# Attention scores of a two-block layer: fp32 matmuls on 32-row strips in place of bf16 stacks through DRAM

## The reference

```python
q, k, v = proj(layernorm(x), Wq, bq), proj(ctx, Wk, bk), proj(ctx, Wv, bv)   # 16 heads of 16
scores = jnp.clip(einsum('bhsd,bhtd->bhst', q, k) / 4, -50, 50)
scores = jnp.where(attend, scores, -10000.0)                                # then clipped to -50
probs = softmax(scores);  ctx = einsum('bhst,bhtd->bhsd', probs, v)
x = x + tanh(g) * layernorm(0.05 * (ctx @ Wo.T + bo))
```

## Time and profile before

| | |
|---|---|
| median of 3 runs | 513.97 us (513.65, 513.97, 520.17) |
| span of the profiled execution | 516.7 us, from the first to the last instruction |
| its own time | not listed apart; of the three runs only 520.17 us is above the span |
| TensorE matmul, weight loads | 366.7 us (71%), 247.4 us (48%) |
| VectorE, ScalarE, GpSimd | 364.3 us (71%), 191.3 us (37%), 154.6 us (30%) |
| mean granted TensorE clock | 0.867 |
| chain that ended last | TensorE 36%, VectorE 33%, issue 14%, ScalarE 7%, DMA 5% |

### The profile page before, as it was taken

The page is one execution under the profiler, slowest core; times in us unless marked ns, Lnnn a source line. Parts: engine busy times, 40 slices in busy tenths (PEclk is TensorE's granted clock), DMA queues, the critical chain, the costliest instruction groups (busy, mean ns, idle before and its releaser), DMA issues.

```text
span 516.7 us, 6750 instructions
## 1 busy us (share of the span) xinstructions
PE 366.7 (71%) x2192; PEld 247.4 (48%) x2192; DVE 364.3 (71%) x887; ACT 191.3 (37%) x336; POOL 154.6 (30%) x150
## 2 busy tenths in 40 slices
PE   4664965628998859795975788797686468660665
PEld 2342542405565648584853556565563235530333
DVE  3174875395653498988788656754998697789895
ACT  2333752222441412251334445453201658721231
POOL 5058058100002544554622541212601220030230
PEclk9796997756999998997998899998977879977685
DMA  8499999930111121330498491364100192000001
GB/s 193 134 139 167 148 189 262 266 52 0 42 27 35 62 82 29 94 120 3 119 187 175 92 165 59 59 105 87 18 0 1 47 150 30 2 1 0 20 11 51
DMA packets 47009, 44.20 MB, mean 86 GB/s; under 512 B 6304, under 2 KB 45952, under 8 KB 46976
## 3 DMA queue, kind: packets, MB, share of 16 engines
q1 hardware_dynamic: 44768, 40.53, 38.6%
q0 software_dynamic: 1152, 2.20, 1.8%
q10 hardware_dynamic: 1056, 1.05, 0.7%
HBM read 36.43 MB, written 7.34 MB: 85 GB/s over the span
## 4 chain that ended last, share of the span: by engine, by line
PE 36%; DVE 33%; issue 14%; ACT 7%; DMA 5%; POOL 3%; SPq 1%; DVEq 0%; ACTq 0%; POOLq 0%
PE bank L848 9%; PE bank L874 5%; PE bank L776 4%; DMA probs<-in_L_xattn_Wq 3%; PE bank L733 2%; DVE probs L1264 2%; DVE tok L1223 2%; PE bank L984 2%; PE bank L948 2%; DVE mxraw L1552 2%; DVE mam L1394 2%; DVE probs L1479 1%; PE bank L896 1%; PE bank L810 1%; DVE st L1208 1%
## 5 line engine op out<-in xcount | busy, mean ns | idle before, releaser
L874 PE MATMUL bank<-wexp,wT 128*128 128x256 f32 x192 | 56.1, 420 | 10.1 <-DVE x L1386 10.0
L848 PE MATMUL bank<-tok_r,probs_r 128*128 128x512 f32 x104 | 47.1, 453 | 10.2 <-DVE wT L1375 7.0
L1264 DVE TENSOR_SCALAR probs<-probs,hi 128x512 f32<-128x512 f32 x64 | 32.8, 564 | 28.8 <-ACT probs L1045 28.8
L1097 ACT ACTIVATE silu_sb<-bank 128x512 f32<-128x512 f32 x32 | 19.1, 598 | 86.2 <-PE bank L848 86.2
L659 POOL TENSOR_TENSOR wexp_r<-wexp,probs_r 128x1024 fp32r<-128x1024 f32 x13 | 31.3, 2405 | 58.6 <-ACT probs_r L1056 58.5
L874 PEld LDWEIGHTS bank<-wexp,wT 128*128 128x128 f32 x192 | 38.4, 211 | 17.6 <-issue 12.4
L1045 ACT ACTIVATE probs<-bank 128x1024 f32<-128x1024 f32 x32 | 32.3, 1027 | 38.2 <-PE bank L760 38.2
L584 POOL TENSOR_TENSOR mx_grid<-parts,bl 128x1024 bf16<-128x1024 fp8e4 x9 | 17.2, 1910 | 96.1 <-DVE parts L1555 96.1
L1479 DVE SCALAR_TENSOR_TENSOR probs<-bank,dexp 128x384 f32<-128x384 f32 x48 | 26.5, 555 | 21.7 <-PE bank L934 15.9
L848 PE MATMUL bank<-tok_r,wexp_r 128*128 128x512 f32 x104 | 41.7, 401 | 0.0
L569 POOL TENSOR_TENSOR mxraw<-mxraw,mx_grid 128x512 f32<-128x512 f32 x12 | 15.3, 1275 | 63.8 <-DVE mx_grid L1420 63.8
(11 more groups left out here) (243 smaller groups left out, 923.0 us busy)
## 6 DMA issues: line engine op xcount, KB each, us to landing
krep<-part_dram SPq DMA_DIRECT2D x64, 128.0 KB, 6.4
qrep<-part_dram SPq DMA_DIRECT2D x64, 128.0 KB, 6.7
wexp<-in_L_ffn_W SPq DMA_DIRECT2D x28, 256.0 KB, 4.4
part_dram<-parts SPq DMA_DIRECT2D x12, 384.0 KB, 3.6
wexp<-in_L_ffn_Wg SPq DMA_DIRECT2D x14, 256.0 KB, 4.4
part_dram<-parts POOLq DMA_DIRECT2D x4, 384.0 KB, 8.1
x<-in_x ACTq DMA_DIRECT2D x2, 512.0 KB, 9.6
ctx<-in_ctx SPq DMA_DIRECT2D x2, 512.0 KB, 9.7
```

The source lines that it names most:

```text
L848: mm = pe.matmul(bank[:, bk, :], lhs, rhs, start=(kk == 0 and q == 0), stop=(kk == KC - 1 and q == len(terms) - 1))
L874: mm = pe.matmul(bank[:, 2 + pair, D * t:D * t + D], hid[k % 2][m][:, col:col + P], wexp[:, k % WR, 2, m, :], start=(m == 0), stop=(m == 1))
L1097: act.activation(silu_sb[:, w % 2, :], bank[:, 0, :], ACT.Silu if direct else ACT.Tanh, scale=1.0 if direct else 0.5).then_inc(s["sigmoid_ ...
L1264: ins = v.tensor_scalar(w, w, hi[:, 2 * b + kc:2 * b + kc + 1], EM50, ALU.min, ALU.max)
```

## The change

The scores of the first block are fp32 matmuls on 32 of the array's rows. A 32-row strip holds two heads. The keys are written twice (`krows`, parity 0 and 1), each time with the other head's 16 rows multiplied by 0, so that a contraction over 32 rows gives one head; the queries (`qrows`) are written once. A unit takes the same-parity heads of two neighbouring strips, and its four matmuls alternate between the two strips and their banks. ScalarE writes the two key copies from PSUM with a mask as its scale and a masked bias; VectorE writes the queries in one operation. The masks (`kmask`) and the masked biases (`bkm`) are made by VectorE in a new function ahead of its first step. The bf16 split of the first block, its stores and its stacks are gone, and SyncE has no part in `project` any more. `probs` keeps its layout by head; a unit's two heads are now two apart (`score_probs`). The context's split on GpSimd waits for the turns' copies and the clamps of unit 11 in place of the stores.

```diff
+        def score_probs(u):
+            g, jj = u // 4, u % 4
+            heads = probs[:, g % 2, :, :].rearrange("p (r a) t -> p a r t", a=2)
+            return heads[:, jj % 2, 2 * (jj // 2):2 * (jj // 2) + 2, :]
 ...
 (SyncE)
-            def project(u):
-                pair, which, signal = u // 2, (1, 0)[u % 2], ("k_stored", "q_stored")[u % 2]
-                sp.wait_ge(s["split_done"], u + 1)
-                if pair:
-                    sp.wait_ge(s[signal], 16 * pair)
-                sp.dma_start(part_dram[which, pair]..., parts[:, u % 4, :, :]).then_inc(s[signal], 16)
-                if u % 2 == 1 and pair < 2:
-                    stack_pair(pair)
             def score(u):
-                if u in (8, 16):
+                if u == 8:
                     sp.wait_ge(s["scores_done"], u)
-                    stack_pair(u // 8 + 1)
-                if u == 8:
                     for k in range(WR):
                         load_expert(k, (0, 1, 2))
 ...
 (GpSimd)
-            gp.wait_ge(s["split_done"], 8)
+            gp.wait_ge(s["evacuated"], 8)
+            gp.wait_ge(s["clamp_done"], 12)
             for u in range(4):
 ...
-                if u == 0:
-                    gp.wait_ge(s["k_stored"], 64)
-                    gp.wait_ge(s["q_stored"], 64)
 ...
 (TensorE, project)
-                claim(4 + u % 2, "proj_high", u + 1)
+                claim(4 + u % 2, *(("query_rows", u // 2 + 1) if kind else ("key_rows", u + 2)))
 (TensorE, score)
-                pe.wait_ge(s[f"k_stacked{g // 2}"], 128)
-                pe.wait_ge(s[f"q_stacked{g // 2}"], 128)
-                slot = (g // 2) % 2
-                for hh in range(2):
-                    claim(bk + hh, "exp_done", u + 1)
-                    j = 2 * jj + hh
-                    for kc in range(2):
-                        m = pe.matmul(bank[:, bk + hh, S * kc:S * kc + S],
-                                      krep[:, slot, j, col + P * kc:col + P * kc + P], qrep[:, slot, j, col:col + S],
-                                      start=True, stop=True)
+                pe.wait_ge(s["key_rows"], 2 * (g // 2) + 2)
+                pe.wait_ge(s["query_rows"], g // 2 + 1)
+                for q in range(2):
+                    claim(bk + q, "exp_done", u + 1)
+                for kc in range(2):
+                    for q in range(2):
+                        strip = slice(32 * (2 * (jj // 2) + q), 32 * (2 * (jj // 2) + q) + 32)
+                        m = pe.matmul(bank[:, bk + q, S * kc:S * kc + S],
+                                      krows[strip, jj % 2, c, S * b + P * kc:S * b + P * kc + P],
+                                      qrows[strip, c, S * b:S * b + S], start=True, stop=True)
 ...
 (ScalarE, project; odd u: nothing)
-                act.activation(projf[:, u % 2, :], bank[:, 4 + u % 2, :], ACT.Identity, bias=...)
-                act.activation(parts[:, u % 4, 0, :], bank[:, 4 + u % 2, :], ACT.Identity, bias=...)
+                for parity in range(2):
+                    act.activation(krows[:, parity, c, HALF * n:HALF * n + HALF], bank[:, 4, :], ACT.Identity,
+                                   bias=bkm[:, parity, c:c + 1], scale=kmask[:, parity:parity + 1]).then_inc(s["key_rows"], 1)
 (VectorE, project; even u: nothing)
-                k = seq.add(v.tensor_tensor(mt[:, u % 2, :], projf[:, u % 2, :], parts[:, u % 4, 0, :], ALU.subtract))
-                k = seq.add(v.tensor_copy(parts[:, u % 4, 1, :], mt[:, u % 2, :]))
-                v.tensor_tensor(parts[:, u % 4, 2, :], mt[:, u % 2, :], parts[:, u % 4, 1, :], ALU.subtract)
+                v.tensor_scalar(qrows[:, c, HALF * n:HALF * n + HALF], bank[:, 5, :], bqk[:, 1, c:c + 1], None,
+                                ALU.add).then_inc(s["query_rows"], 1)
+            def key_masks():
+                v.wait_ge(s["idf_made"], 1)
+                strips = identf[:, :].rearrange("p (r a d) -> p a r d", a=2, d=HD)
+                for parity in range(2):
+                    seq.add(v.tensor_reduce(kmask[:, parity:parity + 1], strips[:, parity, :, :], AX.XY, ALU.add))
+                v.wait_ge(s["qkb_loaded"], 32)
+                seq.wait()
+                seq.add(v.tensor_scalar(bkm[:, 0, :], bqk[:, 0, :], kmask[:, 0:1], None, ALU.mult))
+                v.tensor_scalar(bkm[:, 1, :], bqk[:, 0, :], kmask[:, 1:2], None, ALU.mult).then_inc(s["kmask_made"], 1)
+                seq.wait()
+                v.wait_ge(s["kmask_made"], 1)
 ...
+            key_masks()
             for name, i in plan:
```

More of the change, by code:

```diff
@@ L280, in flamingo_layers @@
         qrep = sb("qrep", [P, 2, HC, HALF], BF16)
-        projf = silu_sb
         parts = sb("parts", [P, 4, 3, HALF], BF16)
@@ L287, in flamingo_layers @@
         wraw = probs[:, 1, HC // 2:HC, :].rearrange("p h t -> p (h t)").rearrange("p (w r d) -> p w r d", w=4, r=KC)
+        krows = krep[:, :, :, :].rearrange("p a h t -> p (a h t)").bitcast(F32).rearrange("p (a c t) -> p a c t", a=2, c=KC)
+        qrows = qrep[:, :, :, :].rearrange("p a h t -> p (a h t)").bitcast(F32)[:, 0:KC * NT * P].rearrange("p (c t) -> p c t", c=KC)
         mxraw = sb("mxraw", [P, 2, 512])
@@ L308, in flamingo_layers @@
         bqk = sb("bqk", [P, 2, KC])
+        kmask = sb("kmask", [P, 2])
+        bkm = sb("bkm", [P, 2, KC])
         arows = sb("arows", [P, 4, D])
@@ L394, in flamingo_layers @@
         names += [f"{n}_loaded{i}" for n in ("wg", "w2") for i in range(WR)]
-        names += [f"{n}_stacked{u}" for n in "kq" for u in range(8)]
+        names += [f"{n}_stacked{u}" for n in "kq" for u in range(4)]
         s = {n: sem(n) for n in names}
@@ L515, in q_split @@
                 sp.wait_ge(s[f"q_split{u % 2}"], u // 2 + 1)
-                store_parts(sp, 2, u, "cq_stored", u + 1)
+                store_parts(sp, 0, u, "cq_stored", u + 1)
                 if u >= 2:
                     sp.wait_ge(s["qk_done"], 16 * (u - 1))
-                stack_load(sp, qrep, u % 2, 2, u, Q_TERM, s[f"q_stacked{4 + u}"])
+                stack_load(sp, qrep, u % 2, 0, u, Q_TERM, s[f"q_stacked{u}"])
             def ln_in(k):
@@ L532, in cell_values @@
                     u = (g + 3) // 2
-                    stack_load(sp, krep, u % 2, 3, u, K_TERM, s[f"k_stacked{4 + u}"])
+                    stack_load(sp, krep, u % 2, 1, u, K_TERM, s[f"k_stacked{u}"])
             def last(i):
@@ L537, in last @@
                 sp.dma_start(out_dram[:, i, :], x[:, i, :]).then_inc(s["out_stored"], 16)
-            steps = dict(project=project, score=score, up=up, out=out, mx_quantise=mx_quantise, q_split=q_split, ln_in=ln_in,
+            steps = dict(score=score, up=up, out=out, mx_quantise=mx_quantise, q_split=q_split, ln_in=ln_in,
                          cell_values=cell_values, last=last)
@@ L929, in cell_score @@
                 claim(bk, "c_done", w + 1)
-                pe.wait_ge(s[f"k_stacked{4 + g // 2}"], 128)
-                pe.wait_ge(s[f"q_stacked{4 + g // 2}"], 128)
+                pe.wait_ge(s[f"k_stacked{g // 2}"], 128)
+                pe.wait_ge(s[f"q_stacked{g // 2}"], 128)
                 slot = (g // 2) % 2
@@ L1020, in project @@
             def project(u):
-                kind, c = u % 2, u // 2 % 2
+                n, c = u // 4, u // 2 % 2
+                if u % 2 == 1:
+                    return
                 if u == 0:
-                    act.wait_ge(s["qkb_loaded"], 32)
+                    act.wait_ge(s["kmask_made"], 1)
                 act.wait_ge(s["projected"], u + 1)
[L1025 to L1031, removed]
+                for parity in range(2):
+                    act.activation(krows[:, parity, c, HALF * n:HALF * n + HALF], bank[:, 4, :], ACT.Identity,
+                                   bias=bkm[:, parity, c:c + 1], scale=kmask[:, parity:parity + 1]).then_inc(s["key_rows"], 1)
             def tanh(_):
@@ L1044, in score @@
                     act.wait_ge(s["pv_done"], g - 1)
-                act.activation(probs[:, g % 2, 2 * jj:2 * jj + 2, :], bank[:, bk:bk + 2, :], ACT.Exp,
+                act.activation(score_probs(u), bank[:, bk:bk + 2, :], ACT.Exp,
                                scale=1.0 / float(np.sqrt(HD))).then_inc(s["exp_done"], 1)
@@ L1226, in project @@
             def project(u):
-                v.wait_ge(s["proj_high"], u + 1)
-                v.wait_ge(s["proj_copied"], u + 1)
-                k = seq.add(v.tensor_tensor(mt[:, u % 2, :], projf[:, u % 2, :], parts[:, u % 4, 0, :], ALU.subtract))
-                seq.wait(k)
-                k = seq.add(v.tensor_copy(parts[:, u % 4, 1, :], mt[:, u % 2, :]))
-                seq.wait(k)
-                v.tensor_tensor(parts[:, u % 4, 2, :], mt[:, u % 2, :], parts[:, u % 4, 1, :], ALU.subtract).then_inc(s["split_done"], 1)
+                if u % 2 == 0:
+                    return
+                n, c = u // 4, u // 2 % 2
+                v.wait_ge(s["projected"], u + 1)
```

(2 more changed lines are left out.)

18 lines of the change are left out of this document (6 added, 12 removed).

## The result

The changed kernel takes 523.78 us (median of 4 runs, 523.25 to 524.57) against 516.23 us beside it: ratio 1.0108, with an interval of 1.0063 to 1.0153. It is a little slower, within the 2% that were called no change, and on the side and near the size that were forecast. The ratio is 5.6 us, the two medians lie 7.5 us apart: four runs of the kernel before scatter over 6.5 us (513.65 to 520.17), and 13 to 21 runs of it beside the experiments have medians of 518.4 to 519.4 us. The profiled execution's span went from 516.7 to 521.5 us, 4.8 more; the sum had 4.3 more.

What follows compares the result with a forecast made beforehand. Bound: TensorE, ScalarE and VectorE alternating from 45 to 92 us, VectorE alone from 102.27 to 117.83, TensorE from 126 to 162. Terms -4.0 + 8.3 = +4.3 us; against the median of 513.97, 518 us, range 502 to 538.

Steps and rivals of the forecast that it cites:

- the sum: All terms together: -4.0 + 8.3 = +4.3 us against the profiled execution's span of 516.7.
- The unit's price: First attention's scores: a unit alone takes 1.26 us instead of 0.43 to 0.44, two adjacent ones 2.12.
- the switch: TensorE going in and out of strip mode around score units: 0.40 us, bounds 0 and 0.6.
- The head: Start to first scores: 41.1 instead of 45.39, 4.3 us ahead; some 9 without the wait for biases in front.
- GpSimd's split: Context split, some 21 us from about 71: covers clamps of units 12 to 15; group 3's values start at 83.0.
- The middle: From group 3's values to the first output projection and beyond: 4.0 us ahead, between 11.5 ahead and 1.3 behind.
- the row at half clock: Half-clock end of the stretch before the first output projection: ready at 93.9, 1.3 us behind.
- The dense stage: Units 22 to 31 among the first experts' matmuls: +8.3 us, covered by nothing; bounds +4.3 and +17.
- Rival 1: Score units: strips don't overlap, a unit takes 2.12 us, 544 us in all; chance 0.16.
- Rival 2: Score units: weight loads lie open inside a unit, which takes 1.95 us, 537 us in all; chance 0.08.
- Rival 3: Clock recovers: full to 130 us, 11.5 ahead instead of 4.0, switch nearly free; 507 or 503 us; chance 0.18.

Runs made afterwards that it cites:

- e6: The changed kernel with both heads of a unit taken from the same 32-row strip: 564.79 us, 1.0879 of the kernel before.
- e7: The changed kernel with keys and queries in bf16, still on masked 32-row strips, two at once: 0.9822 of the kernel before.
- e1: The changed kernel with VectorE making the masked biases only after normalising x's first half, masks alone staying in front: 1.0042 of the kernel before.
- e5: The changed kernel with GpSimd's split of the context no longer waiting for the clamps of unit 11: 1.0125 of the kernel before.
- e2: The changed kernel with a unit doing both key blocks of one strip before those of the other: 1.0133 of the kernel before.

## Why the prediction was right

**The unit's price** was 1.26 with both switches, and 1.26 was measured between two expert groups (1.07, and 0.10 and 0.09 in the groups beside it). The overlap of two strips, argued from column strips, is shown by e6. So the switch is the 0.40 that was forecast (1.26 less 0.86); in bf16 it is 0.3 (e7).

**The head** was right in each step (scores at 41.1, measured 41.20). e1 shows the cause of the part that was lost: with the masked biases behind x's statistics the first scores start 5.0 us earlier.

**GpSimd's split** covers the clamps of units 12 to 15 as said (4.07 us for four, 0.88 for two in e5 without it), and the values step came at 82.68 instead of 83.0.

**The middle** is the term whose size was off, and the weakest step. The lead at the output projection and beyond was put at 4.0, two fifths of the way between a half and a full clock; that fraction was a guess. Measured: 1.1 at the first output projection, 0.1 at 117.70, and 3.1 more in the dense stage (7.9 worked out, 4.8 seen), 3.2 together. By estimate 2.8 of the 3.1 are the clock: 5.5 us less at half speed are 2.8 us of work. Up to 117 us the row at half clock was the better guide; the lead came almost wholly behind it. That the sum fits within a microsecond is in part luck, since no run varied the clock alone.

**The dense stage** was put at +8.3 and shows 7.9 in TensorE's work. Less 3.2 this is +4.7, the span's +4.8. The absolute forecast of 518 us is 5.8 short of the measured 523.78, most of it because it was built on a median of 513.97 us, which more runs of the kernel before put at 516.23 and later at over 518.

**Rival 1** fell: e6 is what it would have been, and dearer than its 544, at 565. **Rival 2**, loads open inside a unit, fell: the loads take 0.19 us and the pairs still follow after 0.215, once the first has taken 0.32 (four slots in 1.07). Here the trace goes against the Trainium skill's sentence ("TensorE: Matmul & The Clock Gate", Part 3, what overlaps and what doesn't): e6's records on one and the same strip, each with its own load, also follow one another at 0.215, eight in 1.92 less the switch. The same Part 3 of the Trainium skill's page ("The mechanism") also allows a load ahead into a background weight buffer; that is the reading that these rows fit. **Rival 3** fell: the granted clock from 85 to 126 is 0.60, below the 0.66 of the earlier trace rows; only from 120.8 to 129.8 was it above that of the kernel before, and that gave the 3.1 us.

What the prediction didn't see is how large the two halves are that nearly cancel. Without the trip and with bf16 on the same strips the time is 0.9822: the trip through DRAM, with its splits, cost about 9 us, net of the wait for the biases that came with the change, and fp32 on strips costs about 15 against bf16 on strips.

## What to carry to other kernels

A trip through DRAM that makes TensorE idle has to be weighed against the matmul time that it saved: here four fp32 matmuls took the place of four bf16 ones, and in a stage without gaps each added microsecond stood in the end. Fill all four row strips where the banks allow it (1.08 us for what two strips do in 1.93), and put row-strip work beside another engine's chain. Look at what is queued behind a new wait at the front of an engine: the masked biases, two operations of 0.2 us, cost 5.0 us at the first scores and some 3 at the end.

## What was not expected of the hardware

Two fp32 matmuls on different row strips overlap whichever way the loops are written (e2, 1.07 us in both), which matmuls that start strictly in the written order would not give. The clock's level moved with small shifts of the work: it was half at 65.9 to 72.8 us in e1 and at 70.2 to 77.0 in e5, where TensorE had idled 1.0 us at a turn and otherwise worked as in the changed kernel, which idled as long at 69.85 and kept the full clock to 79.9. In e5 this undid what VectorE had gained on the clamps. What sets it there stays open: no run varied it alone, and each kernel has one traced execution.
